# Context stage of a decoder block: unscaled exponentials transposed at a step's end, values ahead of the normalised rows, maxima ahead of the roots

## The reference, cut to what matters

```python
x = x + attn(layernorm(x))                          # self-attention, then its projection
q = layernorm(x)
scores = (q @ Wq.T + bq) @ (ctx @ Wk.T).T / 16      # 77 per token
x = x + softmax(scores) @ (ctx @ Wv.T + bv) @ Wo.T + bo
xn = rmsnorm(layernorm(x)) * norm_weight
probs = softmax(xn @ router_w.T + router_b)         # 8 per token
```

## Time and profile before

| | us |
|---|---|
| median of 3 runs (lowest, highest) | 1180.93 (1179.43, 1181.35) |
| the profiled execution, its own time | 1183.38 |
| its span, first to last instruction | 1181.6 |
| context stage on PE, first projection to the last product with `c_vw` | 788.6 to 900.5 |
| context stage on DVE, to its last instruction | 788.5 to 908.0 |
| first product of the experts | 966.7 |
| busy in the whole span: PE, DVE, ACT, POOL | 1082.7, 1014.3, 767.8, 352.3 |

### The profile page before, as it was taken

The page is one execution under the profiler, slowest core; times in us unless marked ns, Lnnn a source line. Parts: engine busy times, 40 slices in busy tenths (PEclk is TensorE's granted clock), DMA queues, the critical chain, the costliest instruction groups (busy, mean ns, idle before and its releaser), DMA issues. The chain is left out here.

```text
span 1181.6 us, 22857 instructions
## 1 busy us (share of the span) xinstructions
PE 1082.7 (92%) x8540; PEld 596.6 (50%) x8540; DVE 1014.3 (86%) x2168; ACT 767.8 (65%) x932; POOL 352.3 (30%) x316
## 2 busy tenths in 40 slices
PE   7989899999999999999999999999984059999998
PEld 6776333333333333333333333347773048888897
DVE  7998799999999999999999999716998975766663
ACT  4552288788888888888887888864565014655653
POOL 2647822202220221122022000022100022765675
PEclk8987599999999999999999999999997559999999
DMA  7787844514422441443144000036532022554443
GB/s 232 258 252 220 199 74 90 97 23 80 75 52 44 80 78 27 69 79 67 24 84 75 20 12 17 17 105 212 178 107 94 0 72 60 152 147 125 111 112 36
DMA packets 84681, 113.95 MB, mean 96 GB/s; under 512 B 25056, under 2 KB 57568, under 8 KB 84576
## 3 DMA queue, kind: packets, MB, share of 16 engines
q1 hardware_dynamic: 66256, 69.82, 20.0%
q0 software_dynamic: 15024, 36.17, 17.0%
q10 hardware_dynamic: 3296, 6.56, 1.6%
HBM read 73.31 MB, written 38.27 MB: 94 GB/s over the span
## 5 line engine op out<-in xcount | busy, mean ns | idle before, releaser
L811 DVE TENSOR_REDUCE b_max_halves<-banks 128x1 f32<-128x512 f32 x1024 | 626.5, 681 | 13.1 <-PE banks L879 12.9
L748 ACT ACTIVATE b_probs<-banks 128x1024 f32<-128x1024 f32 x512 | 520.4, 1026 | 145.3 <-PE banks L930 145.3
L879 PE MATMUL banks<-b_k,b_q 62*128 62x512 f32 x1024 | 398.4, 469 | 6.0 <-PEq L101 1.5
L930 PE MATMUL banks<-b_q,b_k 64*128 64x512 f32 x1024 | 385.6, 456 | 4.5 <-issue 3.3
L901 PE MATMUL banks<-b_probs,b_v 128*17 128x256 f32 (+1 forms) x3840 | 314.8, 400 | 0.2 <-ACT b_probs L748 0.2
L930 PEld LDWEIGHTS banks<-b_q,b_k 64*128 64x128 f32 x1024 | 157.0, 185 | 224.5 <-issue 170.8
L879 PEld LDWEIGHTS banks<-b_k,b_q 62*128 62x128 f32 x1024 | 161.9, 190 | 40.3 <-DVE b_max_halves L811 38.0
L901 PEld LDWEIGHTS banks<-b_probs,b_v 128*17 128x17 f32 x3840 | 63.9, 95 | 165.1 <-issue 98.5
L551 POOL TENSOR_TENSOR b_att<-b_out,b_rec_spread 128x512 f32<-128x512 f32 x32 | 41.1, 1283 | 310.9 <-DMA b_rec_spread<-reciprocals 310.7
L483 POOL DMA_DIRECT2D b_q<-q_stacks x60 | 31.7, 532 | 226.4 <-PE banks L901 214.3
L1850 DVE TENSOR_TENSOR e_hTl<-e_hT,e_hTh 128x512 fp32r<-128x512 f32 x64 | 47.6, 744 | 48.8 <-ACT e_hT L1604 48.8
(11 more groups left out here) (259 smaller groups left out, 1476.5 us busy)
## 6 DMA issues: line engine op xcount, KB each, us to landing
e_w<-in_w SPq DMA_DIRECT2D x16, 1024.0 KB
q_stacks<-a_parts SPq DMA_DIRECT2D x32, 256.0 KB, 4.2
k_stacks<-a_parts SPq DMA_DIRECT2D x32, 256.0 KB, 4.1
b_q<-q_stacks POOLq DMA_DIRECT2D x30, 256.0 KB, 6.4
b_k<-k_stacks POOLq DMA_DIRECT2D x30, 256.0 KB, 7.2
v_tiles<-a_v ACTq DMA_DIRECT2D x8, 544.0 KB, 3.7
b_rec_spread<-reciprocals SPq DMA_DIRECT2D x128, 32.0 KB, 1.8
attended<-b_att SPq DMA_DIRECT2D x128, 32.0 KB, 2.6
```

The costliest lines, as they stand in the source:

```text
L748: nc.scalar.activation(pr[:, S % NP, u], ps[:, 2 * u:2 * u + 2, :], ACT.Exp, scale=D ** -0.5).then_inc(s_ex[u], 1)
L811: v.tensor_reduce(mxp[:, (k // NB) % 2, s, p, t, kh:kh + 1], ps[:, bank(last), :], AX.X, ALU.max)\
L879: nc.tensor.matmul(ps[:, bank(last), :], qs[g][stack, p, at:at + P], ks[g][stack, p, CH * kh:CH * kh + CH], start=True, stop=True).then_in ...
L930: return nc.tensor.matmul(ps[:, 2 * u + s, :], ks[g][stack, u, P * kt:P * kt + P], qs[g][stack, u, CH * h:CH * h + CH], start=True, stop=True)
```

## The change

Five things change in `cross_attend`:

1. The exponentials are transposed as they are (`c_exp` in place of `c_probs`). The multiplication by the reciprocal sum moves behind the product with the values: `attended` does it together with the addition, in four instructions of 256 columns where `residual` had two of 512. The router terms from `c_vw` get the same factor in `logits`, one instruction more in each of its three calls. `c_probs` and its semaphore go; `c_rec` is kept for all pieces.
2. On PE the transposition of the exponentials stands at the end of the step that made them (`exponentials`), where it was at the start of the next one. The next step begins with the products with the values (`values`), and the transposes of the normalised rows come behind them, both halves together.
3. `project` is cut: its first tile stands between `transposes` and `scores`, its other three behind the scores (in step 1 behind `fold_values`).
4. On ACT the copy of the transposed exponentials comes ahead of `normalise`.
5. On DVE sum and reciprocal (`sums`) stand in the next step, between the first `moments` and `attended`; the scores and their maximum are taken ahead of the aggregation and all of the root.

```diff
@@ ACT @@
             for s in range(NS + 1):
+                if 0 <= s - 2 < J:
+                    act.wait_ge(s_tp, s - 1)
+                    copy(pT[:], ps[0:SK, 2, :]).then_inc(s_tpe, 1)
                 if 0 <= s - 1 < J:
                     j = s - 1
                     act.wait_ge(s_st, s)
                     normalise(xn[:, j % 2], x1[:, j % 3], j, 0, s_na)
-                if 0 <= s - 2 < J:
-                    act.wait_ge(s_tp, s - 1)
-                    copy(pT[:], ps[0:SK, 2, :]).then_inc(s_tpe, 1)
@@ DVE @@
+            def attended(j, a, o):
+                for t in range(NT):
+                    if t % 2 == 0:
+                        dve.wait_ge(s_m2, 2 * j + t // 2 + 1)
+                    ins = v.scalar_tensor_tensor(o[:, t, :], ps[:, (3, 7)[t // 2], C * (t % 2):C * (t % 2) + C],
+                                                 rc[:, j, t:t + 1], a[:, t, :], ALU.mult, ALU.add)
+                    if t % 2:
+                        ins.then_inc(s_m2e, 1)
+                dve.wait_ge(s_m2e, 2 * j + 2)
...
-            def probabilities(j):
+            def sums(j):
                 x = j % 2
                 dve.wait_ge(s_ex, j + 1)
                 chain(v.tensor_reduce(sm[:, x], pe_[:, x], AX.X, ALU.add))
-                chain(v.reciprocal(rc[:, x], sm[:, x]))
-                v.tensor_tensor(pn[:, x], pe_[:, x], rc[:, x].unsqueeze(2).to_broadcast([P, NT, SK]),
-                                ALU.mult).then_inc(s_pn, 1)
+                chain(v.reciprocal(rc[:, j], sm[:, x]))
...
+                v.tensor_tensor(gz[:, n], sc[:, a + 1:b + 1, :, SW:SZ], over(rc[:, n]), ALU.mult)
                 chain(v.tensor_tensor(la[:, n], sc[:, n, :, SK:SW], over(ru[:, n]), ALU.mult))
-                chain(v.tensor_tensor(lb[:, n], lb[:, n], sc[:, a + 1:b + 1, :, SW:SZ], ALU.add))
+                chain(v.tensor_tensor(lb[:, n], lb[:, n], gz[:, n], ALU.add))
@@ PE @@
-            def project(j):
+            def project(j, tiles=range(NT)):
                 q = j % 2
                 pe.wait_ge(s_at[q], 16 * (j // 2) + 16)
-                for t in range(NT):
+                for t in tiles:
...
+            for s in range(NS):
+                if s > 1:
+                    values(s - 2)
+                if 0 < s <= J:
+                    transposes(s - 1)
+                if s + 1 < J:
+                    project(s + 1, (0,))
+                if 0 < s <= J:
+                    scores(s - 1)
                 if s == 1:
                     fold_values()
                     pe.wait_ge(s_voe, 3)
                 if s + 1 < J:
-                    project(s + 1)
+                    project(s + 1, (1, 2, 3))
+                if 0 < s <= J:
+                    exponentials(s - 1)
```

More of the change, by code:

```diff
@@ L1010, in cross_attend @@
         sm = sb("c_sum", [P, 2, NT])
-        rc = sb("c_rec", [P, 2, NT])
-        pn = sb("c_probs", [P, 2, NT, SK])
+        rc = sb("c_rec", [P, J, NT])
         ru = sb("c_spread1", [P, J, NT])
@@ L1040, in cross_attend @@
         s_ex = sem("c_exp_ready")
-        s_pn = sem("c_probs_ready")
         s_nb = sem("c_z_ready")
@@ L1203, in _, with residual @@
             tail.invert(dve, v, LAST, 1)
-            def residual(s, se, j, banks, a, o):
+            def residual(j, a, o):
                 for t in range(0, NT, 2):
[L1208 to L1211, removed]
+                    dve.wait_ge(s_m1, 2 * j + t // 2 + 1)
+                    v.tensor_tensor(o[:, t:t + 2, :], ps[:, 4 + t // 2, :].rearrange("p (t c) -> p t c", c=C),
+                                    a[:, t:t + 2, :], ALU.add).then_inc(s_m1e, 1)
+                dve.wait_ge(s_m1e, 2 * j + 2)
+            def attended(j, a, o):
[7 more added lines that the diff above has]
+                dve.wait_ge(s_m2e, 2 * j + 2)
             def moments(m, a):
@@ L1266, in _ @@
                     dve.wait_ge(s_xb, s + 1)
-                    residual(s_m1, s_m1e, s, (4, 5), xb[:, s % 2], x1[:, s % 3])
+                    residual(s, xb[:, s % 2], x1[:, s % 3])
                     ins = moments(0, x1[:, s % 3])
@@ L1270, in _ @@
                     j = s - 2
+                    sums(j)
                     after(dve, s_so[j % 2], 16 * (j // 2))
                     after(dve, s_nb, j - 1)
-                    residual(s_m2, s_m2e, j, (3, 7), x1[:, j % 3], x2[:, j % 2])
+                    attended(j, x1[:, j % 3], x2[:, j % 2])
                     ins = moments(1, x2[:, j % 2])
                 chain(ins)
+                if 0 <= s - 1 < J:
+                    j = s - 1
+                    w = SZ if j else SW
+                    dve.wait_ge(s_sc, s)
+                    dve.wait_ge(s_kqe, KC + 1)
+                    v.tensor_tensor(sc[:, j, :, 0:w], ps[:, 6, 0:NT * SZ].rearrange("p (t n) -> p t n", t=NT)[:, :, 0:w],
+                                    cb[:, j // 2, 0:w].unsqueeze(1).to_broadcast([P, NT, w]), ALU.add).then_inc(s_sce, 1)
+                    dve.wait_ge(s_sce, s)
+                    v.tensor_reduce(mx[:, j % 2], sc[:, j, :, 0:SK], AX.X, ALU.max, negate=True).then_inc(s_mx, 1)
                 u = slice(0 if first else NT, 2 * NT if second else NT)
@@ L1287, in _ @@
                 guess(v, chain, *root)
[L1288 to L1299, removed]
+                for _ in range(3):
+                    newton(v, chain, *root)
                 v.scalar_tensor_tensor(nm[:, s, u], mv[:, s, u, 0], -1.0, rs[:, s, u], ALU.mult, ALU.mult)\
                     .then_inc(s_st, 1)
-                if 0 <= s - 1 < J:
-                    probabilities(s - 1)
             dve.wait_ge(s_sc, J + 1)
@@ L1369, in idle_products, with values, transposes @@
                     mm(ps[:, 2, 0:C], wp[:, 0, 0:P], wp[:, 0, :], start=True, stop=True)
[L1371 to L1382, removed]
+            at = lambda t: SZ * t
+            def values(j):
+                pe.wait_ge(s_tpe, j + 1)
+                for t in range(NT):
+                    if t % 2 == 0:
+                        after(pe, s_m2e, 2 * j - 1 + t // 2)
+                    last = product(ps[:, (3, 7)[t // 2], C * (t % 2):C * (t % 2) + C],
+                                   [(pT[:, P * t:P * t + P], vo[:, j // 2, :])])
+                    if t % 2:
+                        last.then_inc(s_m2, 1)
+                pe.wait_ge(s_sce, j + 1)
+                for t in range(NT):
+                    last = product(ps[:, 6, at(t) + SW:at(t) + SZ], [(pT[:, P * t:P * t + P], vw[:, j // 2, :])])
+                if j == J - 1:
+                    last.then_inc(s_sc, 1)
+            def transposes(j):
+                pe.wait_ge(s_na, j + 1)
+                if j == 0:
+                    pe.wait_ge(s_kqe, KC + 1)
+                after(pe, s_tne, j)
+                for k in range(KC):
                     for t in range(NT):
@@ L1385, in transposes @@
                                   is_transpose=True, start=True, stop=True)
[L1386 to L1420, removed]
+                last.then_inc(s_tn, 1)
@@ new lines, in scores, with exponentials @@
+            def scores(j):
+                pe.wait_ge(s_tne, j + 1)
+                after(pe, s_sce, j)
+                for t in range(NT):
+                    last = product(ps[:, 6, at(t):at(t) + SW],
+                                   [(xnT[:, k, P * t:P * t + P], kqw[:, j // 2, k, :]) for k in range(KC)])
+                last.then_inc(s_sc, 1)
+            def exponentials(j):
+                after(pe, s_tpe, j)
+                idle_products(7 if j >= J - 2 else 4 if j == 0 else 1)
+                pe.wait_ge(s_ex, j + 1)
+                for t in range(NT):
+                    last = mm(ps[0:SK, 2, P * t:P * t + P], pe_[:, j % 2, t, :], ident[:],
+                              is_transpose=True, start=True, stop=True)
+                last.then_inc(s_tp, 1)
```

## The result

| | median us (lowest, highest), runs | ratio to the kernel before, 95% interval |
|---|---|---|
| before, in that set | 1180.5 (1179.43, 1181.35), 4 | |
| the change | 1197.33 (1192.0, 1201.26), 4 | 1.0137 [1.0116, 1.0158] |
| the change again (`after_again`) | 1191.82 (1190.69, 1193.07), 4 | 1.0098 [1.0083, 1.0114] |
| the change a third time (`after_third`) | 1192.37 (1189.33, 1194.35), 6 | 1.0097 [1.0080, 1.0115] |

Slower, as forecast. The median of the first set, +16.8 us, lies above the range; the two later sets, +12.1 and +11.2, lie within it, and their intervals do not reach that of the first. Medians and ratios leave out one execution of the kernel before (1220.9 us) and one of `transposes_by_tile` (1221.75 us), which were slow as a whole, at a mean clock of 0.82. The profiled execution of the first set (1192.0, span 1190.2) was its fastest.

What follows compares the result with a forecast made beforehand. DVE was taken to set the pace at 11.14 us a step, PE close behind. Stage end 7.0 us later plus 2.9 for the clock gave +9.9, 1190.8 us against the median of 1180.93; range 1185.0 to 1195.0.

Steps and rivals of the forecast that it cites:

- The wait at the start: PE stands still 7.2 us from 804.3, before the first tile of project(2), until the c_attT load lands.
- the clock term: After the standstill PE runs at half speed until 5.9 us after work resumes: +2.9 us, bounds 0 and 3.4.
- near 918: Sign to look for in the new trace: the stage ends on DVE near 918.
- the sum: Whole forecast: 7.0 us later at full clock plus 2.9 us for the clock, +9.9 us.
- PE takes the pace: Middle steps: PE's line of work needs 11.0 us a step where DVE had 11.14; DVE waits some 0.3.
- five steps of 11.02: Middle steps, scores(1) at 832.1 to scores(6) at 887.2, each at PE's 11.02 us.
- the end behind it: After scores(6): c_nm at 891.5, last scores taken by DVE at 898.5, stage ending 7.0 us later at full clock.
- The section on the clock: Start of the stage: the 7.2 us standstill drops PE from 2.4 to 1.2 GHz, costing 2.9 us.
- the statistics row of the same width: DVE middle steps: statistics instructions of 256 columns, 1.41 us, used to size attended at 1.4, so +0.1.
- The 0.9 us that POOL's sums cost DVE before: Four middle steps took 0.9 us over four of 11.14 beside POOL's c_xb; forecast to fall into DVE's slack.
- rival four: POOL's c_xb blocks attended on DVE: up to 2.35 us in three steps, some 1195 us; chance 0.04.
- DVE's own step: Middle steps: 11.14 less 0.40 for c_probs and 0.16 of wait, plus 0.1 for attended, is 10.7 us.

Runs made afterwards that it cites:

- transposes_by_tile: tile_behind_exp with ACT signalling each normalised tile and PE transposing tile by tile; 1177.95 us, 0.9974 of the kernel before.
- the last experiment: Against tile_behind_exp, ACT signals each normalised tile and PE transposes tile by tile, waiting for each; 1177.95 us, 0.9974 of the kernel before.
- after: First profiled execution of the changed kernel, no further edit; 1192.0 us, in a set with median 1197.33 us.
- tile_behind_exp: Changed kernel, step 1's first projection tile behind folding, other steps' last tile behind the exponentials' transposes, idle products cut or moved; 1177.83 us, 0.9979 of the kernel before.

## Why the prediction was right in kind and short in size

- **The wait at the start: right.** Forecast 7.2 us, measured 6.54, 6.76, 6.10, and 6.89 in the kernel before with the same tile moved. With its slow stretch it was priced at 9.6 us to scores(1); the profile shows 8.1, and taking it out of the changed kernel gave 7.2, putting it into the kernel before 9.5. Of the 1.5 too much, 0.7 is the wait and 0.9 the clock term: the clock was back 4 us after work resumed (808.55 to 812.6), not 5.9, so 2.0 in place of 2.9. That the stage ended at 918.2, where "near 918" stood, is luck: this execution began it 2.3 us earlier, and it took 2.6 us more than the sum.
- **PE takes the pace: right.** 11.02 forecast, 11.08 measured, and 10.83 without the idle product (there the loop named below sets it).
- **The step that failed is "five steps of 11.02" and the end behind it, which took 2.4 GHz for granted.** The section on the clock asked only for the standstill of 7.2 us. In the profiles the clock falls in steps 5 and 8 as well: a step of 12.18 us in place of 11.08, and 2.14 us of DVE's wait for the last scores, which the working had as none. That is 3.2 us. With the -1.5 of the start, 0.3 for five steps of 11.08 and 0.6 for `attended` twice at the end (next point) it makes +12.5 where 9.9 stood. What puts the median of the first set another 4 us higher is open (last point).
- `attended` was sized at 1.4 us by the statistics row of the same width; it takes 1.66. The estimate from the Trainium skill (Perfetto Trace Analysis, Optimizing Scalar/DVE Operations) of +0.25 was nearer to the +0.38 measured than the row's +0.1. PE's pace hides it in the middle; it shows at the end, twice.
- The 0.9 us that POOL's sums cost DVE before were to go; they did. The same sums now lie on `attended`, and it keeps its 1.66 beside them: rival four is out.
- The forecast of DVE's own step, 10.7, was right (10.68), in part by luck. `attended` is 0.28 longer than I took it; but the addition that it replaces took 1.46 us in the step, not the 1.28 of the first addition that I read, because PE has its second bank ready only at 866.64 (864.66 + 1.98), and these 0.18 went too:

```profile
865.91 1.46 DVE L1209 TENSOR_TENSOR c_x<-banks,c_x 128x512 f32<-128x512 f32 x2 [0.16 <-PE banks L1317]
```

- Nothing runs at 10.68 without the last experiment: from `c_nm` over normalisation, transposes, copy, scores and roots back to `c_nm` there is a loop of 10.83 us that I had not added up.
- The median of the first set, some 5 us above that of the later two, remains unexplained. Its runs of 1197 to 1201 us have mean clocks of 0.938 to 0.940 against the profiled one's 0.942, but none of them was profiled, and the clock is not all of it: at the same 0.940 one execution of the first set took 1201.26 us and one of `after_again` 1192.3.

## What to carry to other kernels

Before an instruction is moved up on an in-order engine to fill a gap, ask for each of its semaphores what it would find in the first rounds of the pipeline, when the loads are not yet ahead: here one tile, harmless in six steps, waited 6.5 us in one. An order that leaves TensorE with the same work can cost its clock, and one more idle product a step was no safe guard: it left one fall of two. With work that has to be done in the waits (a tile behind the exponentials) the falls were gone and the kernel was faster than before; that run also left out and moved idle products, and no run takes the two apart. When such a change moves the time, cut the rows by granted clock before pricing anything else.

## What the runs showed of the hardware that I had not expected

The clock went to 1.2 GHz with TensorE busy for 43.25 of the 47.8 us before and with no standstill above 0.7 us in them (`after`, at 860.4). In the kernel before, whose waits in a step add up to 1.2 us, longer than the 1.0 us of the changed one, it did not fall in the profile, and neither did it in `tile_behind_exp` at a wait of 1.69 us ahead of the last exponentials:

```profile
887.13 0.66 PE L1423 MATMUL banks<-ident,c_exp 128*77 128x128 f32 x4 [1.69 <-ACT c_exp L1163]
```

The Trainium skill (TensorE: Matmul & The Clock Gate, Why this matters for your kernels) asks for no long gaps between bursts of matmuls. The first stage and the standstill at the start agree; the two falls in the steps come without such a gap.
